# A two-layer window-attention kernel: the plain scores on one PSUM bank instead of two, a fourth spare bank, and new tables of order

## What is computed

```
h = layer_norm(x); windows of 14x14
q, k, v = h @ w_qkv + b_qkv                  # 12 heads x 16
layer 0: q, k turned by rotary embedding
layer 1: attn += rel_h[..., :, None] + rel_w[..., None, :]
attn = softmax(q @ k.T * 16**-0.5);  o = attn @ v
x = x + (gamma *) (o @ w_proj + b_proj)
h = gelu(layer_norm(x) @ w_fc1 + b_fc1)
x = x + (gamma *) (h @ w_fc2 + b_fc2)
```

## Time and profile before

| | us |
|---|---|
| median of 3 runs | 524.78 (522.36 to 525.24) |
| the profiled execution: its own time | 528.78 |
| its span, first to last instruction | 527.0 |
| TensorE busy | 482.8 |
| VectorE busy | 376.7 |
| ScalarE busy | 294.1 |
| GpSimd busy | 179.3 |

### The profile page before, as it was taken

How to read it: one execution, slowest core, us unless ns; L and a number is a source line. 1 busy time by engine, 2 the same in 40 slices (tenths; PEclk the granted TensorE clock), 3 DMA queues, 4 the chain that set the end, 5 groups by cost and what they waited for, 6 DMA issues and landing times.

```text
span 527.0 us, 12656 instructions
## 1 busy us (share of the span) xinstructions
PE 482.8 (92%) x4544; PEld 436.2 (83%) x4544; DVE 376.7 (71%) x910; ACT 294.1 (56%) x632; POOL 179.3 (34%) x259
## 2 busy tenths in 40 slices
PE   8746988799999999999999999899999998889894
PEld 7745876599898989898989898798989896869694
DVE  3957887688588575788989898798989797342320
ACT  0511153274465655677786776758686867556511
POOL 7240515521707262625142341616152404030120
PEclk9887698989799999999999999999999999988799
DMA  7657324811102030203022224213031222200000
GB/s 197 122 106 101 79 52 104 164 47 47 46 22 67 25 76 17 72 16 69 20 48 46 60 49 91 49 34 62 26 67 34 63 48 62 48 19 8 8 16 15
DMA packets 33476, 30.33 MB, mean 58 GB/s; under 512 B 6688, under 2 KB 31784, under 8 KB 33416
## 3 DMA queue, kind: packets, MB, share of 16 engines
q1 hardware_dynamic: 31688, 26.72, 23.6%
q10 hardware_dynamic: 1728, 2.81, 1.9%
HBM read 7.84 MB, written 1.57 MB: 18 GB/s over the span
## 4 chain that ended last, share of the span: by engine, by line
PE 69%; SPq 9%; issue 7%; DMA 7%; DVE 3%; ACT 2%; POOL 2%; ACTq 1%; POOLq 0%; DVEq 0%
PE ps L1138 17%; PE ps L1344 11%; PE ps L1266 6%; PE ps L1289 6%; PE ps L1212 6%; DMA QT<-mT 5%; SPq L411 4%; PE ps L1185 4%; PE ps L1321 2%; PE ps L1178 2%; PE ps L1239 2%; PE ps L1301 2%; PE ps L1228 2%; PE ps L1194 2%; SPq L381 1%
## 5 line engine op out<-in xcount | busy, mean ns | idle before, releaser
L910 ACT ACTIVATE PT<-ps 98x392 f32<-98x392 f32 x192 | 93.3, 494 | 98.3 <-PE ps L1266 97.6
L741 DVE TENSOR_REDUCE mneg<-ps 98x2 f32<-98x392 f32 x192 | 105.1, 558 | 32.6 <-PE ps L1212 31.5
L1212 PE MATMUL ps<-KM,QT 128*98 128x196 f32 x384 | 70.8, 269 | 20.2 <-DMA QT<-SPL 8.6
L1266 PE MATMUL ps<-QT,KM 128*98 128x196 f32 x384 | 84.6, 304 | 4.7 <-DMA QT<-mT 3.5
L1212 PEld LDWEIGHTS ps<-KM,QT 128*98 128x98 f32 x384 | 52.1, 175 | 23.2 <-DMA QT<-mT 9.3
L1344 PE MATMUL ps<-W,GT 128*128 128x192 f32 x384 | 65.9, 328 | 1.0 <-ACT GT L953 0.9
L1138 PE MATMUL ps<-WQ,XHa 128*128 128x384 f32 (+2 forms) x320 | 62.1, 306 | 4.2 <-DVE XHa L629 4.0
L1266 PEld LDWEIGHTS ps<-QT,KM 128*98 128x98 f32 x384 | 55.3, 171 | 12.3 <-DMA QT<-mT 4.4
L1138 PE MATMUL ps<-XHm,WF 128*128 128x256 f32 x384 | 62.8, 290 | 1.2 <-DVE XHm L629 1.2
L1344 PEld LDWEIGHTS ps<-W,GT 128*128 128x128 f32 x384 | 62.0, 190 | 1.9 <-ACT GT L953 1.5
L993 POOL TENSOR_SCALAR vepsm<-mvm 128x2 f32<-128x2 f32 x16 | 3.1, 192 | 171.8 <-DVE mvm L608 171.8
(11 more groups left out here) (149 smaller groups left out, 1015.8 us busy)
## 6 DMA issues: line engine op xcount, KB each, us to landing
KM<-SPL SPq DMA_DIRECT2D x96, 96.0 KB
QT<-SPL SPq DMA_DIRECT2D x96, 96.0 KB
X<-in_x SPq DMA_DIRECT2D x8, 94.5 KB
out<-X SPq DMA_DIRECT2D x8, 94.5 KB
W<-in_w ACTq DMA_DIRECT2D x1, 576.0 KB, 6.3
W<-in_w SPq DMA_DIRECT2D x1, 576.0 KB, 6.2
QT<-mT SPq DMA_DIRECT2D x28, 6.0 KB
raw<-in_w ACTq DMA_DIRECT2D x1, 384.0 KB, 3.2
```

Source lines behind the costliest of these rows:

```text
L741: v.tensor_reduce(mneg[n % 2][0:CH, 0:2 * NH].rearrange("p (t h) -> p t h", t=2)[:, :, h], bank[0:CH, 0:2 * NM].rearrange("p (t k) -> p t ...
L910: a.activation(PT[:, at % (2 * GROUP), :], ps[0:CH, ST_BANK + h % 2, 0:2 * NM], ACT.Exp)\
L1212: last = mm(ps[0:CH, S_BANK + h % 2, NM * t:NM * t + NM], QT[p][:, h, CH * t:CH * t + CH], KM[p][:, h, 0:NM], start=True, stop=True)
L1266: last = mm(ps[0:CH, ST_BANK + h % 2, NM * c:NM * c + NM], KM[p][:, h, CH * c:CH * c + CH], QT[p][:, h, 0:NM], start=True, stop=True)
```

## The change

The plain scores lose one of their two banks. All heads use bank 0, the weighted values move from bank 4 to bank 1, the transposed scores stay on 2 and 3, and the spare banks are 4 to 7, four instead of three. The scores of a head now wait for the maximum of the head just before. The tables USES, WORK, SETUP, ONCE and MOVES have new numbers throughout.

```
-        S_BANK, ST_BANK, O_BANK, MISC, NMISC = 0, 2, 4, 5, 3
+        S_BANK, ST_BANK, O_BANK, MISC, NMISC = 0, 2, 1, 4, 4
...
-            {"stats": -157, "inv_std": -140, "xn": -119, "xe": -140, "cosine": -99, "sine": -95, "rotate": -90,
+            {"stats": -153, "inv_std": -130, "xn": -95, "xe": -140, "cosine": -103, "sine": -83, "rotate": -92,
...
-                bank = ps[:, S_BANK + h % 2, :]
+                bank = ps[:, S_BANK, :]
...
-                if NH * n + h >= 2:
-                    pe.wait_ge(e.mneg, NH * n + h - 1)
+                if NH * n + h >= 1:
+                    pe.wait_ge(e.mneg, NH * n + h)
                 for t in range(2):
-                    last = mm(ps[0:CH, S_BANK + h % 2, NM * t:NM * t + NM], QT[p][:, h, CH * t:CH * t + CH],
+                    last = mm(ps[0:CH, S_BANK, NM * t:NM * t + NM], QT[p][:, h, CH * t:CH * t + CH],
```

More of the change, by code:

```diff
@@ L191, in build @@
         USES = (
[7 rows of a table removed]
[7 rows of a table added]
         )
         WORK = (
-            {"stats": -157, "inv_std": -140, "xn": -119, "xe": -140, "cosine": -99, "sine": -95, "rotate": -90,
[L203 to L207, removed]
[3 rows of a table removed]
-        )
@@ L213, in build @@
[L213 to L221, removed]
+            {"stats": -153, "inv_std": -130, "xn": -95, "xe": -140, "cosine": -103, "sine": -83, "rotate": -92,
+             "out0": 29, "out1": 37, "out2": 51, "xb": 70, "mstats": 78, "minv": 103, "mxn": 104, "mxb": 105,
+             "gelu0": 101, "gelu1": 101, "gelu2": 101, "pk0": -79, "pq0": -70, "pk1": -47, "pq1": -65,
+             "row": -21},
[5 rows of a table added]
+        )
@@ new lines, in build @@
+        ONCE = {"f0": 4, "wa": 75, "wb": 75, "f1": 138, "bk": 192}
+        SETUP = {"pads": -116, "bv0": -97, "values0": -96, "keys": -75, "scales0": -2, "fc00": 2, "fc01": 41,
+                 "scales1": 48, "lnb1": 70, "fc10": 103, "fc11": 105, "bare": 109, "values1": 149, "qkv1": 155,
+                 "clear": 225, "img3": -97, "img4": -65, "img5": -12, "img6": -9, "img7": 57, "w1": 58,
+                 "wp1": 405, "w21": 487}
+        MOVES = {("prepare", 1): -10, ("mlp", 14): 19, ("attend", 8): -2, ("attend", 9): -2,
+                 ("attend", 13): -1, ("attend", 11): -2, ("attend", 12): -2, ("attend", 0): -5,
+                 ("attend", 14): -1, ("attend", 7): 1, ("attend", 4): 1, ("mlp", 12): -1, ("prepare", 3): -1,
+                 ("attend", 15): -1, ("attend", 10): -2, ("attend", 5): 1, ("prepare", 0): -1,
+                 ("attend", 6): 1, ("mlp", 15): 3, ("mlp", 7): 1, ("mlp", 6): 1}
@@ L1366, in keep_clock @@
                 for _ in range(products):
-                    mm(ps[:, S_BANK + 1, 0:128], ones[:], ones[:], start=True, stop=True)
+                    mm(ps[:, S_BANK, 0:128], ones[:], ones[:], start=True, stop=True)
             pe.wait_ge(S.ones, 1)
```

## The result

The changed kernel takes 541.1 us (535.5 to 542.0, four runs) against 525.0 us (522.4 to 527.6) of the kernel before: a ratio of 1.027, 95% interval 1.021 to 1.033. The forecast was 530.3, and 541.1 is above the range's end of 537.5. A second set of six runs, made with the experiments (e9), gave 535.4 us and a ratio of 1.018 (1.013 to 1.022). So the change costs about 10 us in one set of runs and 16 in the other. Within a set the time goes with TensorE's granted clock: 535.5 us at 0.946 and 541.4 at 0.932 in the first.

What follows compares the result with a forecast made beforehand. TensorE's own work was taken to bound the kernel from step 3 to step 14. Terms 2.6 + 3.5 - 2.5 + 0.9 + 1.0 + 0 = +5.5 us on a 524.8 median gave 530.3 us, range 520.5 to 537.5.

Steps and rivals of the forecast that it cites:

- the loop's lengths: One bank's round trip, the least distance of two heads: 1.09 us at full clock, 1.28 at the lower level.
- (a): Rival: the loop is hidden, its waits falling where DMA waits stood; sum 0, some 525 us; chance 0.18.
- (b): Rival: faster, 2.5 us from the bank and 4 from DMA waits at step beginnings; 519 us; chance 0.15.
- (c): Rival: VectorE becomes the bound in layer 1, late maxima stalling TensorE, start losing 4.8; 538 us; chance 0.17.
- Term 1: Start, step 0's to step 2's first head: short intervals lengthened to a round trip, 4.8 less 2.2 given back; +2.6 us.
- The chain of SP: Before step 3: SP's unbroken jobs from step 1's maxima to step 3's queries, same jobs and order after the change.
- Term 2: Layer 0, steps 3 to 6: heads wait for maxima, 4.5 us less 1.0 of earlier row waits; +3.5 us.
- Term 3: Fourth spare bank: users after 105 us find their bank free a turn earlier, ending nine short waits; -2.5 us.
- Term 4: Load of W2 in step 11: head 6 waits 2.3 us in place of 1.8, plus 0.4 queued behind; +0.9 us.
- Term 5: Last two steps, 14 and 15: heads again stand closer than 1.09 us in four intervals; +1.0 us.
- Term 6: Layer 1: VectorE's work spread over the MLP intervals, TensorE never more than 0.1 us late; 0.
- some forty: Sign of being right: plain scores wait for maxima in some forty places rather than 5, most ahead of step 7.

Runs made afterwards that it cites:

- e9: The changed kernel itself, run again unaltered for a second trace and more times; 535.4 us, ratio 1.018 to the kernel before.
- e3: The changed kernel's new order with the old banks, two for the plain scores and three spare; 559.5 us, ratio 1.065.
- e10: The changed kernel with unread products, fewer to fit the gaps, ahead of eight start heads and a step 2 projection, waits kept; 532.5 us, ratio 1.014.
- e15: The changed kernel with 30 unread products ahead of step 0's first head and nothing else; 537.8 us, ratio 1.021.
- e1: The kernel before, old order and three spare banks, with one bank for the plain scores; 564.6 us, ratio 1.069.
- e6: The changed kernel with unread products ahead of 8 heads of steps 0 and 1 and a step 2 projection, waits kept; 540.6 us, ratio 1.027.

## Why the prediction was wrong

**Right:** slower, with waits for maxima mostly at the start (though I had put the larger term on layer 0); the loop's lengths (1.28 to 1.31 us at the lower level, 1.05 to 1.09 at the upper; a few heads stand 1.00 apart); that nothing behind the start gives its loss back; that layer 1 loses nothing to maxima; W2 now hits head 6 instead of head 0; rivals (a) and (b) fall, and (c), whose 538 lies nearer than my 530, has the wrong mechanism: from step 7 to 10 no head waits for a maximum, and the loss lies elsewhere.

**Term 1, the start, is the step that failed: +2.6 against +9.8 and +10.9.** Three things are wrong in it. First, 2.2 us were given back for a projection and the bias sums that "stood elsewhere" and would use gaps. The bias sums stood in the same 24 heads before, at 53.32, ahead of head 11 of step 0; there was nothing to give back for them. The projection of v did come in, from 32.4, ahead of the first head; it now stands at 44.51 to 46.17 at the lower clock and sets heads 2 and 3 2.11 us apart, more than the loop, so it costs time there instead of filling a gap. In before, the projection, then the bias sums and heads 11 and 12; in the changed kernel, heads 2 and 3 with the first rows of the projection:

```profile
32.39 0.25 PE L1138 MATMUL ps<-WQ,XLa 128*98 128x192 f32 x1
...
53.32 0.30 PE L1111 MATMUL ps<-lnp,raw 128*128 128x1 f32 x2
...
56.97 0.88 PE L1212 MATMUL ps<-KM,QT 128*98 128x196 f32 x4
```

```profile
44.06 0.65 PE L1213 MATMUL ps<-KM,QT 128*98 128x196 f32 x2
44.51 0.37 PE L1139 MATMUL ps<-WQ,XHa 128*98 128x192 f32 x1
...
46.17 0.54 PE L1213 MATMUL ps<-KM,QT 128*98 128x196 f32 x2
```

Second, only intervals shorter than a round trip were counted (4.8; measured 5.2 to 6.3 by e3 against after), and not what else the new tables move at the start, such as the projection of step 2 that waits 1.17 us for VectorE at 57.63: e3 puts 4.6 on the order, all of it longer busy time (57.48 against 52.80 us). Third, every piece was priced at the clock of the old trace. Filling gaps in e10 takes 4.9 us of the total back by the clock; since the first two are measured as times, this lies within them and does not add. Step 3 began at 115.1 (107 forecast). The chain of SP did what the prediction said, but it starts behind step 1's maxima (their row is issued at 89.14, before at 78.50) and so passes on all 10 us; at its end TensorE idles 0.71 us, where it had idled 3.3. SP's row of step 1's maxima, then step 3's first head, in the changed kernel:

```profile
89.14 0.79 SPq L421 DMA_DIRECT2D QT<-mT  x1
```

```profile
115.08 0.42 PE L1213 MATMUL ps<-KM,QT 128*98 128x196 f32 x2 [0.71 <-DMA QT<-mT]
```

**Term 2, steps 3 to 6: +3.5 against +0.7** (the first trace's +3.7 agrees by chance: its clock was 0.93 there). In step 5 the third head came 2.26 us after the first, 2.45 forecast, and the transposed scores began 3.83 after it, 3.55 before. These rows of the changed kernel answer to the earlier trace rows:

```profile
176.70 0.34 PE L1213 MATMUL ps<-KM,QT 128*98 128x196 f32 x2
...
177.70 0.42 PE L1213 MATMUL ps<-KM,QT 128*98 128x196 f32 x2
...
178.96 0.43 PE L1213 MATMUL ps<-KM,QT 128*98 128x196 f32 x2 [0.65 <-DVE mneg L742]
...
180.53 0.43 PE L1267 MATMUL ps<-QT,KM 128*98 128x196 f32 x2
```

The waits were about right and the net was not: step 5 took 26.2 us, not 27, with TensorE busy for 25.55 of them where it had been for 25.03 of 26.1, so the step's gaps shrank instead of growing. That the projection pushed out of this stretch fills gaps later in the step is the likely reason, but no run separates it.

**Term 3, the fourth bank: -2.5 forecast, and steps 7 to 10 are 4.5 us shorter, 1.7 of it the wait of step 11's first head.** The remaining 2.8 are near the forecast by luck, since the working fails: with the old order a fourth bank gives 0.3, with the new one its absence costs 14. It was priced as a resource under a fixed order, while it is a condition of the new order.

**Term 4, W2: +0.9 against +2.1 to +5.0 for step 11 in the two traces (+0.7 in e15), and -1.7 for head 0 of it, net +0.4 to +3.3.** The wait of head 6 was forecast at 2.3 and measured at 2.38 in one trace, 3.55 in the other; the clock behind it was left out.

**Term 5, the end: +1.0 forecast.** Heads wait 0.2 us for maxima behind step 6 (12.4 less 10.2 at the start and 2.0 in steps 3 to 6), and the part from step 12 on is 1.7 us shorter; which change of order does that was not tried. The sign was wrong.

**Term 6, layer 1: 0, and 0.** e1 shows what that rests on: with the old order the same loop costs 8 us in steps 7 to 10, which is rival (c).

The places that wait for a maximum are 23, not some forty. And 541.1 lies above the range because the start's bound was 5 and the start lost 9.8 to 10.9.

## What to carry to other kernels

A plan of banks and a table of order are one design. Here the banks alone cost 38 to 40 us and the order alone 33, and the two together 10 to 16; a term that prices a bank under the old order says nothing of its worth in an order made for it. Where TensorE already waits often, as at a pipeline's start, price an order by its busy time too: further short gaps cost once as gaps, and once more as the work behind them at the lower clock. Before crediting moved work with filling gaps, look up where it stood in the old trace.

## What the runs showed of the hardware

With no gap longer than 1.3 us from 42 to 76 us, and gaps of 0.3 to 1.3 ahead of half of the heads there, TensorE's granted clock stood at 0.50 over most of 52 to 76 us; filling these gaps with products of 0.12 us each raised the clock of steps 0 to 2 from 0.79 to 0.84 and shortened them by 4.9 us. Two banks without this filling (e3) left it at 0.79. A product of 128x128 in this kernel is two instructions, 0.12 us each at the upper level and 0.23 at the lower, so that a count taken for one per product doubled the dose in e6. And the same kernel's two traces differ by 6.6 us of span with almost the same waits for maxima (12.4 and 12.2 us in 18 places): the stretches at the lower level behind the start did not fall in the same places in the two.
